# One fused attention and FP4 feed-forward kernel: GpSimd's jobs reordered, weight work spread over other steps, a first half of the keys loaded by ScalarE's queue, four score pairs taken into the prologue

## The reference

```python
x = x + xattn(layernorm(x), ctx)
#   q, k, v = x @ Wq.T + bq, ctx @ Wk.T + bk, ctx @ Wv.T + bv   (16 heads of 16)
#   softmax(q @ k.T / 4) @ v @ Wo.T + bo
xq, wq = fp4(x), fp4(w)      # scale = max|.| / 6 over 16 columns, values on the FP4 grid
h = silu(fp4(layernorm(x)) @ fp4(w_gate).T) * (fp4(layernorm(x)) @ fp4(w_up).T)
x = x + fp4(h) @ fp4(w_down).T
```

## Time and profile before

| | |
|---|---|
| time, median of 3 runs | 1806.91 us (1804.79 to 1809.01) |
| the profiled execution | 1806.17 us, its span 1804.4 us |
| TensorE busy | 1666.5 us, 92% of the span |
| VectorE busy | 1422.4 us, 79% |
| ScalarE busy | 1131.0 us, 63% |
| GpSimd busy | 562.2 us, 31% |

### The profile page before, as it was taken

The page is one execution under the profiler, slowest core; times in us unless marked ns, Lnnn a source line. Parts: engine busy times, 40 slices in busy tenths (PEclk is TensorE's granted clock), DMA queues, the critical chain, the costliest instruction groups (busy, mean ns, idle before and its releaser), DMA issues.

```text
span 1804.4 us, 26956 instructions
## 1 busy us (share of the span) xinstructions
PE 1666.5 (92%) x9408; PEld 660.9 (37%) x9408; DVE 1422.4 (79%) x2077; ACT 1131.0 (63%) x2293; POOL 562.2 (31%) x673
## 2 busy tenths in 40 slices
PE   5798889999998999989999999989999899989958
PEld 2332234334432344333443334423343334323325
DVE  5778888878786887969788788878879697798447
ACT  2366667666676667666676666766677666666731
POOL 4327530532126220343205421162202532012204
PEclk8899999999998999999999999999999999999979
DMA  6644332232324313252331423243132422300000
GB/s 157 145 77 124 71 74 43 67 95 51 61 43 115 79 39 59 48 123 52 63 55 50 106 57 61 43 106 81 38 57 57 93 46 49 57 7 10 13 21 12
DMA packets 106482, 117.51 MB, mean 65 GB/s; under 512 B 23140, under 2 KB 87660, under 8 KB 106348
## 3 DMA queue, kind: packets, MB, share of 16 engines
q1 hardware_dynamic: 101808, 111.93, 29.3%
q10 hardware_dynamic: 4540, 3.87, 0.9%
HBM read 76.78 MB, written 30.16 MB: 59 GB/s over the span
## 4 chain that ended last, share of the span: by engine, by line
PE 77%; DVE 10%; ACT 5%; issue 4%; POOL 1%; DMA 0%; SPq 0%; ACTq 0%; POOLq 0%; DVEq 0%
PE pvb L824 20%; PE st L795 19%; PE mx L809 10%; PE misc L725 7%; PE misc L697 5%; DVE cmx L1051 4%; PE misc L690 4%; ACT prob L976 3%; PE misc L745 3%; PE misc L737 2%; PE misc L676 2%; PE misc L711 1%; PE misc L733 1%; PE misc L766 1%; DVE ht L1080 1%
## 5 line engine op out<-in xcount | busy, mean ns | idle before, releaser
L976 ACT ACTIVATE prob<-st 128x512 f32<-128x512 f32 (+1 forms) x1584 | 863.7, 599 | 385.3 <-PE st L795 382.8
L1051 DVE TENSOR_REDUCE cmx<-mx 128x2 f32<-128x1024 f32 x768 | 905.7, 1219 | 216.1 <-PE mx L809 212.8
L795 PE MATMUL st<-qstack,kstack 112*128 112x512 bf16 (+1 forms) x1584 | 500.0, 389 | 53.8 <-ACT prob L976 44.0
L824 PE MATMUL pvb<-prob,vv 128*32 128x512 f32 (+1 forms) x3328 | 446.9, 609 | 0.6 <-ACT prob L976 0.6
L795 PEld LDWEIGHTS st<-qstack,kstack 112*128 112x128 bf16 (+1 forms) x1584 | 128.6, 99 | 516.3 <-issue 247.0
L809 PE MATMUL mx<-kstack,qstack 48*128 48x512 bf16 (+1 forms) x2048 | 255.6, 339 | 29.5 <-DVE cmx L1051 16.4
L1306 POOL TENSOR_TENSOR ht<-ht,rh 128x352 f32<-128x352 f32 (+1 forms) x78 | 57.3, 759 | 462.2 <-DVE rh L1027 462.2
L725 PE MATMUL misc<-wguT,rowsT 128*128 128x352 f32 x456 | 154.3, 460 | 0.0
L1298 POOL TENSOR_TENSOR ht<-ht,mt 128x352 f32<-128x352 f32 (+1 forms) x140 | 124.6, 913 | 74.1 <-DVE mt L1208 60.7
L809 PEld LDWEIGHTS mx<-kstack,qstack 48*128 48x128 bf16 x2048 | 58.2, 94 | 203.4 <-issue 134.3
L1312 POOL TENSOR_TENSOR cin<-cin 128x400 f32<-128x400 f32 (+1 forms) x60 | 58.3, 972 | 233.2 <-ACT cin L916 233.2
(11 more groups left out here) (182 smaller groups left out, 1556.7 us busy)
## 6 DMA issues: line engine op xcount, KB each, us to landing
kstack<-scr_k SPq DMA_DIRECT2D x384, 100.1 KB, 4.3
scr_k<-cin SPq DMA_DIRECT2D x48, 300.0 KB, 3.9
qstack<-scr_q SPq DMA_DIRECT2D x372, 32.0 KB, 1.8
cin<-ctx_in SPq DMA_DIRECT2D x16, 512.0 KB, 5.3
scr_q<-qp SPq DMA_DIRECT2D x16, 384.0 KB, 4.5
scr_k<-cin SPq DMA_DIRECT2D x16, 300.8 KB, 4.9
xn<-x SPq DMA_DIRECT2D x8, 512.0 KB, 4.0
cin<-ctx_in SPq DMA_DIRECT2D x16, 256.0 KB, 5.5
```

The source lines that it names most:

```text
L795: mm(score_bank(it, n, h)[0:KROWS[kt], :], kstack[:, hd, KOFF[kt]:KOFF[kt] + KROWS[kt]], qstack[:, hd, :], start=True, stop=True).then_inc ...
L824: last = mm(pvb[2 * D * h:2 * D * (h + 1), :], vv[0:w, kt, (HG * g + h) // 2, D * (h % 2):D * (h % 2 + 2)], prob[0:w, n % 2, h, :], start= ...
L976: activate(prob[0:KROWS[kt], n % 2, 2 * pair + h, :], score_bank(it, n, 2 * pair + h)[0:KROWS[kt], :], ACT.Exp, scale=SCALE).then_inc(exp_ ...
L1051: v.tensor_reduce(cmx[:, g % 2, h0:h0 + 2, at:at + 1], products, op=ALU.max, axis=AX.X).then_inc(max_free, 1)
```

## The change

Five edits. (1) `POOL_WORK`: the splits of k2 and k3 stand ahead of `xround` 0, and the split of q1 ahead of `xround` 1. (2) The weights in "first": VectorE's search for the maxima becomes a step of its own, GpSimd's steps get tables of their own, and pieces and transposes stand in other steps. (3) In the prologue the lead of the first group's keys is loaded in two halves: columns 0 to 800 by ScalarE's queue, between the lead and the rest of the queries, after only two of the four pieces are in DRAM; the other columns by SP as before. The pairs of a group go through the query tiles for one bank of 512 keys before they go to the next bank, so that the first four pairs need only the first half. (4) Four pairs of the second group are taken in steps 48 and 49 of the prologue, and "first" takes three pairs a step in 6 steps and not in 10. (5) In a step without a shared job on the first side, the first pair stands between the two halves of the scores.

```diff
-CATCH_UP = 2 * M_LEAD - M_GROUP
+AHEAD = 4
+CATCH_UP = 2 * M_LEAD - M_GROUP - AHEAD
...
-W_SCALE_AT = {17: 0, 19: 1, 28: 2, 31: 3, 38: 4, 41: 5}
-W_POWER_AT = {20: 0, 22: 1, 30: 2, 33: 3, 40: 4, 43: 5}
+W_AMAX_AT = {12: 0, 14: 1, 24: 2, 27: 3, 33: 4, 39: 5}
+W_SCALE_AT = {13: 0, 15: 1, 25: 2, 28: 3, 34: 4, 40: 5}
+W_POWER_AT = {17: 0, 20: 1, 26: 2, 31: 3, 37: 4, 42: 5}
+W_SCALED_AT = {14: 0, 16: 1, 25: 2, 28: 3, 34: 4, 40: 5}
+W_ROUND_AT = {18: 0, 20: 1, 26: 2, 31: 3, 37: 4, 42: 5}
 POOL_WORK = {
-    0: [("late", "bias", 0)], 10: [("early", "k", 0)], 11: [("early", "k", 1)], 12: [("early", "q", 0)], 13: [("late", "xround", 0), ("early", "k", 2)],
-    14: [("early", "k", 3)], 15: [("early", "k", 4)], 16: [("late", "xround", 1), ("early", "q", 1)], 17: [("early", "k", 5)], 18: [("early", "k", 6)], 19: [("early", "k", 7)],
+    0: [("late", "bias", 0)], 10: [("early", "k", 0)], 11: [("early", "k", 1)], 12: [("early", "q", 0), ("early", "k", 2)], 13: [("early", "k", 3)],
+    14: [("late", "xround", 0), ("early", "k", 4)], 16: [("early", "q", 1), ("late", "xround", 1)], 17: [("early", "k", 5)], 18: [("early", "k", 6)], 19: [("early", "k", 7)],
...
+            if it.kind == "pre":
+
+                first, last = (first, M_GROUP) if n < STEPS - M_LEAD + M_HEADS else (first - 2, M_GROUP + AHEAD)
+                if not (n != STEPS - M_LEAD + M_HEADS and first < last):
+                    return []
...
+                            k0 = COFF[2] if it.kind == "pre" and g == rest == 0 else 0
+                            sp.dma_start(kstack[row:row + D, HG * g + par:HG * (g + 1):2, k0:T],
+                                         src[:, HG * g + par:HG * (g + 1):2, a, k0:T]).then_inc(k_stack[g][rest], 16)
...
+                    if j == 0 and it.kind == "pre" and g == 0:
+                        pe.wait_ge(k_first, BLOCKS)
+                    if j == (QT if it.kind == "pre" and g == 0 else 0):
+                        pe.wait_ge(k_stack[g][0], it.count(part, BLOCKS, BLOCKS))
...
-                    t, n = divmod(piece, FULL)
+                    n, t = divmod(piece, QT)
...
+                    products = maxima(it, n)
+
+                    between = 1 if has_att and not jobs(it, n, 0) else 0
+                    for job in products[:between]:
+                        pair_products(job)
                     if has_att:
                         scores(n, 1)
-                    products = maxima(it, n)
-                    for job in products[:2]:
+                    for job in products[between:2]:
                         pair_products(job)
...
+                        if rest == 0:
+                            for n in range(2):
+                                act.wait_ge(k_out[n], 16)
+                            for par in range(2):
+                                for j, a in enumerate(K_PARTS[0]):
+                                    row = HALF * par + D * j
+                                    act.dma_start(kstack[row:row + D, par:HG:2, 0:k1], keys[:, par:HG:2, a, 0:k1]).then_inc(k_first, 16)
```

More of the change, by code:

```diff
@@ L92 @@
     20: ([("gate", 0, "late"), ("bob", 0, "once")], []),
-    21: ([("gate", 1, "late")], [("nm", 2, "att")]),
-    22: ([("up", 0, "late")], []),
+    21: ([("gate", 1, "late"), ("wT", 0, "once")], [("nm", 2, "att")]),
+    22: ([("up", 0, "late"), ("wT", 1, "once")], []),
     23: ([("up", 1, "late")], []),
-    24: ([("gate", 2, "late"), ("wT", 0, "once")], []),
-    25: ([("gate", 3, "late"), ("wT", 1, "once")], []),
+    24: ([("gate", 2, "late"), ("wT", 2, "once")], []),
+    25: ([("gate", 3, "late"), ("wT", 3, "once")], []),
@@ L98 @@
     26: ([("up", 2, "late")], []),
-    27: ([("up", 3, "late"), ("wT", 2, "once")], [("hqT", 0, "late")]),
-    28: ([("gate", 4, "late"), ("wT", 3, "once")], [("hqT", 1, "late")]),
+    27: ([("up", 3, "late")], [("hqT", 0, "late")]),
+    28: ([("gate", 4, "late")], [("hqT", 1, "late")]),
     29: ([("down0", 0, "late")], []),
-    30: ([("down", 0, "late")], []),
-    31: ([("gate", 5, "late")], []),
+    30: ([("down", 0, "late"), ("wT", 4, "once")], []),
+    31: ([("gate", 5, "late"), ("wT", 5, "once")], []),
@@ L104 @@
     32: ([("up", 4, "late")], [("hqT", 2, "late")]),
     33: ([("up", 5, "late")], [("hqT", 3, "late")]),
[L106 to L110, removed]
+    34: ([("gate", 6, "late")], [("nm", 3, "att")]),
+    35: ([("down0", 1, "late"), ("wT", 6, "once")], []),
@@ L111 @@
+    36: ([("down", 1, "late"), ("wT", 7, "once")], []),
+    37: ([("gate", 7, "late")], [("hqT", 4, "late")]),
+    38: ([("up", 6, "late")], [("hqT", 5, "late")]),
     39: ([("up", 7, "late")], []),
-    40: ([("down0", 2, "late")], []),
-    41: ([("down", 2, "late")], []),
+    40: ([("down0", 2, "late"), ("wT", 8, "once")], []),
+    41: ([("down", 2, "late"), ("wT", 9, "once")], []),
     42: ([("v", 0, "early")], []),
-    43: ([("v", 1, "early")], [("hqT", 6, "late"), ("wT", 8, "once")]),
@@ L116 @@
-    44: ([("v", 2, "early")], [("hqT", 7, "late"), ("wT", 9, "once")]),
-    45: ([("down0", 3, "late")], []),
-    46: ([("down", 3, "late")], []),
+    43: ([("v", 1, "early")], [("hqT", 6, "late")]),
+    44: ([("v", 2, "early")], [("hqT", 7, "late")]),
+    45: ([("down0", 3, "late"), ("wT", 10, "once")], []),
+    46: ([("down", 3, "late"), ("wT", 11, "once")], []),
     47: ([("v", 3, "early")], [("nm", 0, "early")]),
-    48: ([("v", 4, "early")], [("wT", 10, "once")]),
-    49: ([("v", 5, "early")], [("wT", 11, "once")]),
+    48: ([("v", 4, "early")], []),
@@ L122 @@
+    49: ([("v", 5, "early")], []),
     50: ([("v", 6, "early")], []),
@@ L408, in maxima @@
             if it.kind == "first" and n < CATCH_UP:
-                first, number = M_GROUP + 3 * n, 3
-            if part not in it.parts or it.kind == "pre" and first >= M_GROUP:
+                first, number = M_GROUP + AHEAD + 3 * n, 3
+            if it.kind == "pre":
+                first, last = (first, M_GROUP) if n < STEPS - M_LEAD + M_HEADS else (first - 2, M_GROUP + AHEAD)
+                if not (n != STEPS - M_LEAD + M_HEADS and first < last):
+                    return []
+            if part not in it.parts:
                 return []
@@ L962, in first_queries @@
                     act.wait_ge(q_out, 16)
-                    src = scr_q.rearrange("(h i) a n -> i h a n", i=D)
+                    src, keys = (scr.rearrange("(h i) a n -> i h a n", i=D) for scr in (scr_q, scr_k))
+                    k1 = COFF[2]
                     for rest in range(2):
```

21 lines of the change are left out of this document (11 added, 10 removed).

## The result

The changed kernel takes 1744.67 us (median of 4 runs, 1743.73 to 1745.13); the kernel before took 1807.05 us beside it. The ratio is 0.9655, with an interval of 0.9638 to 0.9671. The prediction was 1743 us, with 8 chances in 10 for 1732 to 1760.

A forecast was written before the change was run, and what follows sets the result against it. TensorE, busy 92% of the span, bounds the kernel; some 58 us hang on GpSimd's order. Savings of 52, 7, 2.5, 1 and 0.5 us (edits 1, 2, 4, 3, 5) sum to 63: 1806.2 to 1743 us, range 1732 to 1760.

The forecast's parts named there:

- The reading of the wait: ScalarE's unnamed wait before key pieces k4 and k7 is for GpSimd's splits, queued behind roundings awaiting VectorE; some 58 us.
- The 6 us held back: Six loops: 1 us each taken off the 58 us for a late `xround` 1, leaving 52 us saved.
- What is late next is `xround` 1, by VectorE: Loops, before k7: the k5 split, behind `xround` 1, ends between 0.4 us early and 1.2 us late.
- the first wait goes, with almost 4 us to spare: Loops, before k4: k2's split is done at 334.2, ScalarE wants k4's turn at about 338.
- a sign of being wrong: Loops: a wait over 2 us left at k7, or TensorE waiting for VectorE's reductions in steps 13 to 18.
- The rule's price: `xpower` 1 in the loops: three instructions each wait up to 0.95 us for GpSimd; saving some 41 us, not 52.
- the 82 of the sum: "first", steps 19 to 41: VectorE's 74 us plus some 8 us of unevenness gives 82 us, against 90 before.
- the bound of 1.5: Prologue, first keys loaded in halves: the rests landing earlier moves the end by between 0 and 1.5 us.
- A: Loops, before k7: the second wait stays as VectorE finishes `xpower` 1 late; 1755 us, or 1762 if all; chance 0.17.
- B: First batch gains nothing: transposes catch up with GpSimd's rounding or a raw weight piece comes late; 1750 us; chance 0.08.
- C: Loops: ScalarE's unnamed wait is for something else than GpSimd's order; 1795 us, or no gain; chance 0.03.
- D: Loops: late `xround` 1 holds `xlast` 1 ahead of the pairs, stopping TensorE once a loop; slower, 1815 us; chance 0.02.

## Why the prediction was right

It was right in the whole for its main reason: edit 1 is nearly four fifths of the gain, by the wait that was named. That the sum came so close, 61 us of span for 63, is in part luck: edit 1 gave 4 us less than its term and edit 2 1.5 more, and the terms of edits 3 and 5 are smaller than what one kernel differs from the next.

- **The reading of the wait** holds. The chain and the timeline put 58 us on GpSimd's order; with edit 1 undone 47 come back, and the unnamed wait with them.
- **Edit 1: 52 us predicted, 48.1 by the trace, 46 to 47 by the medians.** The 6 us held back, 1 a loop, should have been 1.6 a loop. And they stand elsewhere. "What is late next is `xround` 1, by VectorE" was half the answer: at k7 0.5 us is left (step 19, 4.58 for 4.07). The other 1.2 us stand in step 14, where the prediction had "the first wait goes, with almost 4 us to spare" and looked no further. That k3's split, moved there, would run beside `xpower` 0, and that TensorE would then wait for pairs, was not in the sum. It stood only in the last line, as a sign of being wrong, and that sign has come: TensorE waits for VectorE's reductions in step 14. It cost 1.2 us a loop, inside the bounds of the term. k4 to k5 took 9.47 us by the timeline and not 8.4, for the same reason.
- **The lock.** The Trainium skill ("SBUF — State Buffer", "Who interferes with whom") has VectorE and GpSimd shut one another out for a whole instruction. The trace agrees: a 0.43 us instruction ended 0.27 to 0.29 us after GpSimd's, at 1.13 and 0.96. The rule's price, 2.9 us on the second wait and so 41 us for the edit, was too high for that place: of the three instructions of `xpower` 1 one met GpSimd (L1195, 1.26 us for 0.43). Three more met it in steps 11 and 12, where the prediction had not looked. Each of the four lost 0.5 to 0.8 us, and TensorE saw 1.2 us of it in step 14 and 0.5 at k7. The same section says that a reduction on this chip never contends, and the pairs, 2.36 us for two beside a busy GpSimd or not, agree.
- **Edit 2: 7 predicted, 8.5 by the trace** (7.6 and 0.9), 9.7 by the spans with it undone. The steps came to 82.04 us, the 82 of the sum, though in the sum 82 had stood there without the new wait. The wait was foreseen, at 1 to 2 us, and was 1.79. That it must be subtracted was wrong: with it gone, the time stayed. Of the 9.7 us 1.0 stands in the tail, where the edit changes nothing.
- **Edit 4: 2.5 predicted, 1.9 in the steps**, 4.5 by the medians. A little under half of the 4.7 us of reductions came back; half was assumed. The rest of the 4.5 is not explained.
- **Edit 3: 1 predicted.** The first pair is 4.7 us earlier (33.52; the prediction had worked out 35.3, 2.9 earlier), and the key matmul 1.85 (a microsecond was expected). What reaches the end is not settled: 0 by the one trace without it, 3 by the medians, which is above the bound of 1.5, with a scatter of 2.7 between equal prologues.
- **Edit 5: 0.5 predicted, 0 measured.** Within its bounds of 1 us either way nothing can be told.
- **The rivals.** A (the second wait stays) would need ScalarE's 3 us at k7 and there are 0.8 above the ordinary. B is refuted by steps 20 to 42, C by edit 1 undone. D has not come: no loop has a stop at `xlast` 1.

## What to carry to other kernels

When an in-order engine's wait has no named releaser, look in the code for what it waits for and on the engine that owes it for what is ahead in its list: the cure was to put what others wait for ahead of what itself has to wait. Before a moved job is booked at zero, lay it beside what VectorE runs at that moment, and count the meetings both where the job goes and where the jobs behind it go. And a wait that you remove at an engine near full can give nothing if a second engine was catching up during it. Two edits here took 1.2 and 2.4 us out of one step, and later steps gave them back.

## What I had not expected of the hardware

- A collision of VectorE and GpSimd is not a slowdown by a factor. The later one ends some 0.14 us less than its own time after the earlier one's end: VectorE's instructions of 0.19 us (L1054, L1058) 0.05 us after GpSimd's, those of 0.43 (L1195, L1196) 0.27 to 0.30 us after, those of 0.68 (L1194, L1216) 0.54 to 0.56 us after, in all loops and kernels read. So 0.43 us became 0.95 to 1.27. It strikes GpSimd too: L1351 on q1, 1.16 us alone, took 1.49 beside L1194 and ended 1.0 us after it.
- After TensorE stood for 1.79 or 2.16 us, the eight matmuls behind took 1.94 us and not 1.07, with the granted clock at 0.83 over the 10 us around. That is nearly the factor between the two levels, 1.2 and 2.4 GHz. But the same wait doesn't always bring it. In step 21 of "first" TensorE stands for 1.8 us in eight kernels; in three of them the clock stays at 1.00 from 156 to 166, and in the others it falls (0.83 in the changed kernel).
- The same prologue, whose first scores the trace has waiting for a DMA, began them anywhere in 2.7 us.
